# Moving one attention layer and several dense node layers to other passes of a fused four-network graph kernel

## What is computed

```python
# L0: graph attention, three layers
x = relu(node_features @ W0 + b0)
for l in range(3):
    # logits = leaky_relu(a_s[src] + a_d[dst] + ew); softmax over the edges of a node
    y = _gat(x, src_f, dst_f, ew_f, Wg[l], att_src[l], att_dst[l], bg[l], n)
    y = _layer_norm(y, gamma[l], beta[l])
    x = jax.nn.relu(x + y)
# L1: two graph convolutions (weighted), relu(agg @ W.T + b)
# L2: one graph convolution, relu(segment_sum(xw[row] * norm) + b)
# L3: two SAGE layers, relu(concat(h, mean of neighbours) @ W + b)
x = _layernorm(x + L0(x));  x = _layernorm(x + L1(x))
x = _layernorm(x + L2(x));  x = _layernorm(x + L3(x))
```

## Time and profile before

| what | value |
|---|---|
| median of 3 runs | 5088.15 us |
| the profiled execution's span | 5076.4 us |
| instructions | 107540 |
| busy: PE / DVE / ACT / POOL | 77% / 75% / 68% / 59% of the span |
| DMA packets | 606699, 1061.18 MB, mean 209 GB/s |
| `node_chain` | 860.9 us, DVE busy 798.2 |
| `edge_scores` 0, 1, 2 | 385.6, 316.8, 365.1 us |
| `convolve` 0, 1, 3 | 273.2, 260.7, 259.0 us |

### The profile page before, as it was taken

How to read it: one execution, slowest core, us unless ns; L and a number is a source line. 1 busy time by engine, 2 the same in 40 slices (tenths; PEclk the granted TensorE clock), 3 DMA queues, 4 the chain that set the end, 5 groups by cost and what they waited for, 6 DMA issues and landing times. The chain is left out here.

```text
span 5076.4 us, 107540 instructions
## 1 busy us (share of the span) xinstructions
PE 3921.6 (77%) x23992; PEld 2865.7 (56%) x23992; DVE 3818.0 (75%) x14850; ACT 3446.1 (68%) x11317; POOL 3017.8 (59%) x2914
## 2 busy tenths in 40 slices
PE   2999999565997798994998974997876676665554
PEld 1666766344775455773555752444765565665554
DVE  5899999676998787887886966997768787444443
ACT  0899999554886576784776863887878787333332
POOL 2888888475552122661223452887757676767777
PEclk9999999788998899997999997998999898997666
DMA  2566666587997576994776984775766566543332
GB/s 63 162 186 199 199 194 193 175 288 242 351 349 250 180 239 205 338 354 160 233 241 230 350 290 156 225 227 171 230 205 212 189 204 190 155 145 116 93 101 70
DMA packets 606699, 1061.18 MB, mean 209 GB/s; under 512 B 109737, under 2 KB 130875, under 8 KB 606509
## 3 DMA queue, kind: packets, MB, share of 16 engines
q1 hardware_dynamic: 524780, 920.61, 53.0%
q0 software_dynamic: 81728, 138.51, 10.7%
HBM read 608.75 MB, written 453.92 MB: 209 GB/s over the span
## 5 line engine op out<-in xcount | busy, mean ns | idle before, releaser
L2534 POOL DMA_INDIRECT got_c<-table,src_row x980 | 930.4, 949 | 387.6 <-issue 295.6
L1428 POOL DMA_INDIRECT src_got_s<-table,src_row x588 | 554.6, 943 | 452.9 <-PE bank L1474 105.1
L2566 PE MATMUL bank<-pick_c,got_c 128*128 128x128 f32 x1960 | 327.7, 319 | 349.6 <-DMA got_c<-table,src_row 271.2
L2076 PE MATMUL bank<-w_all,dt_m 128*128 128x512 f32 x1176 | 567.7, 599 | 35.0 <-DMA dt_m<-delta_t 33.4
L2566 PEld LDWEIGHTS bank<-pick_c,got_c 128*128 128x128 f32 x1960 | 284.2, 223 | 392.5 <-issue 233.5
L2050 POOL TENSOR_TENSOR part_m<-part_m,half_sum_m 128x512 f32<-128x512 f32 x98 | 158.7, 1619 | 580.3 <-DVE half_sum_m L2283 580.3
L1601 ACT ACTIVATE z_s<-z_s,shift_s,dev_s 128x128 f32<-128x128 f32 x1080 | 444.2, 486 | 1.8 <-DVE shift_s L1739 1.3
L791 PEld LDWEIGHTS bank<-w_mean,ht 128*128 128x128 f32 x2352 | 312.4, 193 | 142.9 <-issue 142.9
L2590 PE MATMUL bank<-w_c,agg_c 128*128 128x128 f32 x1960 | 365.4, 311 | 5.0 <-ACT agg_c L2711 4.7
L2711 ACT COPY agg_c<-bank 128x512 f32<-128x512 f32 x245 | 142.6, 582 | 325.4 <-DVE bank L1914 277.8
L788 PE MATMUL bank<-bias,first_row 128*128 128x512 f32 x588 | 321.8, 629 | 38.7 <-ACT ht L851 13.8
(11 more groups left out here) (352 smaller groups left out, 11925.4 us busy)
## 6 DMA issues: line engine op xcount, KB each, us to landing
table<-rows SPq DMA_DIRECT2D x294, 256.0 KB
x_s<-table SPq DMA_DIRECT2D x270, 256.0 KB
x_c<-table SPq DMA_DIRECT2D x245, 256.0 KB
table<-z_s SPq DMA_DIRECT2D x196, 256.0 KB
table<-z_c SPq DMA_DIRECT2D x196, 256.0 KB
table<-mid_s SPq DMA_DIRECT2D x172, 256.0 KB
own_rows_s<-table SPq DMA_DIRECT2D x147, 256.0 KB
pick_t_s<-picks_t SPq DMA_DIRECT2D x147, 256.0 KB
```

The source lines that it names most:

```text
L1428: nc.gpsimd.indirect_dma_start(out=src_got[r][:, g, :], out_offset=None, in_=tables[l].rows, in_offset=bass.IndirectOffsetOnAxis(ap=src_ro ...
L2076: nc.tensor.matmul(b_h[k % n_h][:, :], dt[b.slot][:, k, :], w_all[:, l, :, :].rearrange("p h d -> p (h d)"), start=True, stop=True).then_i ...
L2534: nc.gpsimd.indirect_dma_start(out=got[r][:, g, :], out_offset=None, in_=t_in.rows, in_offset=bass.IndirectOffsetOnAxis(ap=src_row[:, t:t ...
L2566: ins = nc.tensor.matmul(b_sum[r][:, k * P:(k + 1) * P], got[b.slot][:, k, :], pick[r][:, k, :], start=k == 0, stop=sage, skip_group_check ...
```

## The change

1. `node_chain` keeps the input layer and two attention layers. The addition of the old row (`add_rows`) goes from POOL to DVE for both, the bias of layer 1 is now copied into its bank by ACT (`set_bias`) instead of multiplied in by PE, and the steps of all engines are written in a new order with fewer steps between the stages of a batch. POOL issues its 392 node-map DMAs without pacing.
2. The third attention layer of the node rows, with the raw input added and the LayerNorm, goes into `edge_scores(0)` as its pair (`attention=...`, `row_deviation` on ACT, `layer_norm`, `residual`, `moments`, `scale` on DVE); it loads the old rows and the raw rows and writes t[3].
3. The pair of L1's two layers moves from `edge_scores(0)` to `edge_scores(1)`, that of L2's layer from `edge_scores(1)` to `edge_scores(2)`.
4. L3's node batches leave `edge_scores(2)`. All 98 now run in `convolve(0)` to `convolve(3)`: 25, 25, 25 and 23, one in every second pass. `convolve(0)` carries 25 as before.

```diff
+def node_quarters(nb):
+
+    hosted, n = (nb + 1) // 2, 2 * nb
+    starts = [min(k * hosted, n) for k in range(4)] + [n]
+    return list(zip(starts[:-1], starts[1:]))
...
-                        for n in range(n_batches + 7):
-                            if 7 <= n:
-                                add_rows(1, n - 7)
-                            if n < n_batches:
-                                hold(pool, first_made, n - 2)
-                                if n == nb:
-                                    pool.wait_ge(placed, 16 * n_tiles)
-                                map_step(4 * n)
-                            if 4 <= n < n_batches + 4:
-                                add_rows(0, n - 4)
-                            if n < n_batches:
-                                map_step(4 * n + 2)
+                        for t in range(n_tiles):
+                            place(t)
+                        pool.wait_ge(placed, 16 * n_tiles)
+                        for t in range(n_tiles):
+                            fetch(t)
                         pool.wait_ge(fetched, 16 * n_tiles)
 
...
+                        def add_rows(l, b):
+                            r = b.slot
+                            dve.wait_ge(y_read[l], b.count(1, 1))
+                            dve.wait_ge(rows_made[l], b.count(1, 1))
+                            nc.vector.tensor_tensor(flat(rows[l + 1][r]), flat(rows[l + 1][r]), flat(rows[l][r]),
+                                                    ALU.add).then_inc(summed[l], 1)
+
+                        def relu_rows(l, b):
+                            r = b.slot
+                            dve.wait_ge(summed[l], b.count(1, 1))
+                            nc.vector.scalar_tensor_tensor(rows[l + 1][r][:, :, :], rows[l + 1][r][:, :, :], 0.0, beta_k(l + 1), ALU.max,
+                                                           ALU.add).then_inc(made[l + 1], 1)
...
+                                scale(1, b)
+                                add_rows(1, b)
...
+                            if b:
+                                add_rows(0, b)
                                 relu_rows(0, b)
...
-        def edge_scores(l, first, second, t_in, t_mid, t_out, start, end, solo=False):
-            n_part, patch = end - start, l and not start
+        def edge_scores(l, first, second, t_in, t_mid, t_out, attention=None):
+            patch = l > 0
...
+                            if attention:
+                                sp.dma_start(flat(raw[h][b.slot]), batch_rows(io["x"], b.twin(h).batch())).then_inc(raw_in[h][b.slot], 16)
...
+                        def layer_norm(b, h):
+                            n = b.twin(h)
+                            dve.wait_ge(dev_made, n.count(1, 1))
+                            nc.vector.reciprocal(dev_y[h][:, :], dev_y[h][:, :]).then_inc(inverse, 1)
+                            dve.wait_ge(inverse, n.count(1, 1))
+                            hold(dve, z_stored[h][b.slot], b.ring4(16, -16))
+                            dve.sem_inc(dve_pace, 1)
+                            for g in range(GB):
+                                ins = nc.vector.scalar_tensor_tensor(z[h][b.slot][:, g, :], b_y[h][:, g * D:(g + 1) * D],
+                                                                     dev_y[h][:, g:g + 1], gamma_w[:, l + 2, :], ALU.mult, ALU.mult)
+                            ins.then_inc(y_read, 1)
+                            dve.wait_ge(y_read, n.count(1, 1))
+                            nc.vector.tensor_tensor(flat(z[h][b.slot]), flat(z[h][b.slot]), flat(x[h][b.slot]),
+                                                    ALU.add).then_inc(rows_added, 1)
...
+                        def step_attention(at):
+                            b = at(2)
+                            if b:
+                                difference(b)
+                            b = at(1)
+                            if b:
+                                layer_norm(b, 0)
+                                residual(b, 0)
+                                moments(b, 0)
+                            b = at(2)
+                            if b:
+                                scale(b, 1)
+                            b = at(1)
+                            if b:
+                                layer_norm(b, 1)
+                                residual(b, 1)
+                                moments(b, 1)
                                 scale(b, 0)
-                            b = at(2)
...
                 def even(b):
-                    return nodes and b and b.slot % 2 == 0
+                    if not nodes or not b or b.slot % 2:
+                        return False
+                    return not isinstance(b.i, int) or b.batch() // 2 < n_own
+
+                def node_batch(b):
+                    return b.ring(1, first_node - 1)
...
+                            b = at(5)
+                            if even(b):
+                                node_residual(b)
+                                node_moments(b)
+                            b = at(6)
+                            if even(b):
+                                node_scale(b)
...
-        edge_scores(0, (io["L1_gnn_W1"], io["c_L1_gnn_b1"]), (io["L1_gnn_W2"], io["b_L1_gnn_b2"]), t[3], t[4], t[5], 0, nb)
+        edge_scores(0, None, None, t[2], None, t[3], (w_mean[:, 2, :], bias[:, 2, :, :]))
         softmax(0)
         attend(0)
-        edge_scores(1, None, (io["L2_gnn_W"], io["b_L2_gnn_b"]), t[5], None, t[6], 0, nb)
+        edge_scores(1, (io["L1_gnn_W1"], io["c_L1_gnn_b1"]), (io["L1_gnn_W2"], io["b_L1_gnn_b2"]), t[3], t[4], t[5])
         softmax(1)
         attend(1)
-        middle = (nb + 1) // 2
-        third = (t[6], t[7], t[8], (io["L3_gnn_W1"][0:D, :], io["c_L3_gnn_b1"]), (io["L3_gnn_W2"][0:D, :], io["b_L3_gnn_b2"]))
-        edge_scores(2, third[3], third[4], *third[0:3], 0, middle)
-        edge_scores(2, third[3], third[4], *third[0:3], middle, nb, True)
+        edge_scores(2, None, (io["L2_gnn_W"], io["b_L2_gnn_b"]), t[5], None, t[6])
         softmax(2)
         attend(2)
-        convolve(0, "gcn0", False, t[3], t[4], None, (io["L1_gnn_W1"],), io["b_L1_gnn_b1"], third + (2 * (nb - middle) + 1,))
-        convolve(1, "gcn0", True, t[4], t[5], t[3], (io["L1_gnn_W2"],), io["b_L1_gnn_b2"])
-        convolve(2, "gcn1", True, t[5], t[6], t[5], (io["L2_gnn_W"],), io["b_L2_gnn_b"])
-        convolve(3, "sage", False, t[6], t[7], None, (io["L3_gnn_W1"][D:, :], io["L3_gnn_W1"][0:D, :]), io["b_L3_gnn_b1"])
+        third = (t[6], t[7], t[8], (io["L3_gnn_W1"][0:D, :], io["c_L3_gnn_b1"]), (io["L3_gnn_W2"][0:D, :], io["b_L3_gnn_b2"]))
+        quarters = [third + (lo, hi) for lo, hi in node_quarters(nb)]
+        convolve(0, "gcn0", False, t[3], t[4], None, (io["L1_gnn_W1"],), io["b_L1_gnn_b1"], quarters[0])
+        convolve(1, "gcn0", True, t[4], t[5], t[3], (io["L1_gnn_W2"],), io["b_L1_gnn_b2"], quarters[1])
+        convolve(2, "gcn1", True, t[5], t[6], t[5], (io["L2_gnn_W"],), io["b_L2_gnn_b"], quarters[2])
+        convolve(3, "sage", False, t[6], t[7], None, (io["L3_gnn_W1"][D:, :], io["L3_gnn_W1"][0:D, :]), io["b_L3_gnn_b1"], quarters[3])
         convolve(4, "sage", True, t[7], t[8], t[6], (io["L3_gnn_W2"][D:, :], io["L3_gnn_W2"][0:D, :]), io["b_L3_gnn_b2"])
```

530 lines of the change are left out of this document (201 added, 329 removed).

## The result

The changed kernel takes 5452.26 us (median of 4 runs, 5447.98 to 5454.08), the kernel before 5087.38 beside it. The ratio is 1.072, 95% interval 1.0707 to 1.0733. Forecast were 5210 us and a range of 5120 to 5300: the sign was right, the size was not, 365 us slower instead of 122.

The account below looks back on a forecast made before the run. Limits differed by block: busy PE, DVE and ACT in node_chain, transfers in the scores, gathers and almost a DVE-ACT ring in convolve(1). Terms -209 + 124 + 73 - 48 + 85 + 85 + 12 = +122 gave 5210 us, range 5120 to 5300.

Parts of the forecast that it names:

- `node_chain`: Term for this block: 6.35 us per batch by VectorE's list, 652 us in all, -209.
- rival 3: node_chain bound by its round of waits at the lower clock, 7.7 us per batch, total 5348 us; chance 0.12.
- `edge_scores(0)`: Term for this block: VectorE's list sets 10.0 us per pass, 510 us in all, +124.
- `edge_scores(1)` and `(2)`: Terms for these blocks: transfer-bound before and after, 390 us (+73) and 316.75 us (-48).
- `convolve(1)` and `(2)`: Terms for these blocks: node batches enter the DVE and ACT ring, mean 6.37 us per pass, 346 us each, +85 each.
- The ring of the earlier trace: In convolve(1), DVE and ACT wait on each other with nothing spare; with node batches it sets 6.37 us per pass.
- `convolve(3)`: Term for this block: node batches cost fill and drain only, about +12 us.
- 1 and 2: Rivals: everything moved is hidden, 4944 us, chance 0.04; only the convolutions hide, 5068 us, 0.06 shared with the cheap-ends rival.
- the four: All rivals: everything hidden, only convolutions hidden, node_chain's round at lower clock, and all terms at cheap ends together (5055 us).
- The clock, weighed for `node_chain`: With PE idler in node_chain its clock may fall to the lower level, 138 us more than forecast; chance 0.12.

Follow-up runs that it names:

- Experiment 8: GpSimd adds the rows in edge_scores(0) beside VectorE's statistics and aggregation, ACT normalises behind the next squares, against the base: 5124.63 us, 1.0079 of before.
- Experiment 6: VectorE's shift in convolve(1) and (2) one step later, ACT's node steps ahead of its normalisations, against the base: 5215.24 us beside 5218.52.
- experiment 1: In convolve(3) of the changed kernel, ACT sets the bias and copies the sums out ahead of its node steps: 5217.59 us, 1.0262 of before.
- experiment 3: In convolve(0) of the changed kernel, the copy of the sums one step later, as in convolve(3): 5621.14 us (one run).
- experiments 7: GpSimd adds the rows in edge_scores(0) between its gathers, against the base: 5433.28 us; reordered 6402.64 and 6398.35; with VectorE's difference first again 5312.47.
- the base: The changed kernel with ACT's copy of the sums ahead of its node steps in convolve(3): 5218.52 us, 1.0258 of before.

## Why the prediction was wrong, point by point

**`node_chain`: right.** 654 for 652 us. VectorE's hidden-layer add and max, L891, in 300 us of the changed kernel:

```profile
300.00:600.00 300.00, 37.63 (x47) 1.00 0.52 168
```

47 batches, 6.38 us each, for 6.35; at a clock of 0.98 although PE was busy 75% of the block instead of 91%. So rival 3 (round at the lower clock) fell. That it is VectorE's list and not the round beside it was not tried.

**`edge_scores(0)`: the number right, its reason only half.** 511 for 510, 30 passes in 300 us. But the sum took VectorE's 10.0 us as a list with small overlaps and forecast it busy over 90%, and VectorE was busy 434 of 511 us (85%), 8.9 per pass. Experiment 8 brought the pass to 8.0 us by taking 1.4 from the list and 0.6 of waits with it. So some of the 10.0 us was order and not work; that the sum met it was partly luck.

**`edge_scores(1)` and `(2)`: right**, within 5 us, at a DMA share of 0.95 in both, for 0.96 and 0.95 in the blocks whose place they took the earlier trace rows.

**`convolve(1)` and `(2)`: nearly right**, +95 for +85. The period is 6.84 us, worked out from the window below (152/4 = 38 aggregations in 260 us), for 6.37; fill and drain are 20 us, for 34. The intervals between VectorE's reciprocals (L2777, 3801 to 3857 us) are in turn 6.2 and 7.6 us on average, where 5.9 and 6.8 were forecast: the pass that was mis-sized most is the odd one, by 0.8 us. Periods too short by 23 us in all met a fill too long by 14, so the +85 is nearer than its terms.

```profile
3790.00:4050.00 260.00, 14.41 (x152) 0.91 0.68 213
```

The ring of the earlier trace rows was named as the cause. Experiment 6 cut it and gained nothing that can be measured, so the ring was at most one of two bounds. The other is probably ACT's list, 303 busy of 353 us and 223 of 250 in the middle; the forecast had seen ACT only as the ring's partner.

**`convolve(3)`: wrong, and it is the whole miss.** The step that failed reads "DVE 125 and ACT 83 of 259 us leave room, so as in `convolve(0)` the node batches cost fill and drain only". The busy shares did leave room; experiment 1 shows that the batches cost 2 us once the order allows it. What the step left out is the order itself. For `convolve(1)` I had walked round the ring instruction by instruction, for `convolve(3)` I took over the result of another block by its busy times. The two blocks share the code of their node steps but differ in one number, `b = at(2 if sage else 1)`, which stands in the code before (and in where PE's `add_own` stands, which made no ring: with the number alone changed, experiment 3 made it in `convolve(0)`). `convolve(1)` and `(2)` have `at(2)` too, but there ACT copies the sums ahead of its node steps, the order that experiment 1 gave to `convolve(3)`. With ACT's and PE's order of a step side by side the round would have been seen: node product, ACT's node copy, `sums_out`, product, next sums, next node product. Its length could have been summed too, as experiment 3's expectation does for `convolve(0)`: 7.6 us per pass at full clock, up to 10 with the clock that follows; 8.3 were measured there (49 relus start from 3486.7 to 3886.8 us).

**The rivals.** 1 and 2 (all or the convolutions hidden) were refuted by the blocks' own times. None of the four was the one that came: a ring in the block with the most room. The clock, weighed for `node_chain`, fell elsewhere: in `convolve(3)`, where PE stood waiting in every pass, from 0.98 to 0.75. Around the rows shown it is 1.00 while PE ends its node product and stands (4664 to 4668 us), and 0.50, the lower of its two levels, in the product behind a wait (4658 to 4660 and 4670 to 4672). That agrees with "activity releases the throttle" in the Trainium skill ("TensorE: Matmul & The Clock Gate", "Part 1: The HAM clock gate (the "warmup" mystery)"); `node_chain`, where PE became idler and kept 0.98, shows nothing of it. PE's busy share of `convolve(3)` would not have foretold it: 66% before and after. It was a consequence: in experiment 1 it rose to 0.97 with no edit to PE.

## What to carry to other kernels

When work is hosted beside other work, room in busy time is not enough. Write the step of each engine down in order and look for a pair of engines that wait for each other within one step; if there is one, the pass takes the sum of both sides, however idle both are. The cure is one step of distance, or the short thing that others wait for ahead of the thing that waits. And when a new order makes all engines idler at once and the clock falls with them, look for the ring first: here the clock came back by itself once the ring was cut. When a period is taken from a count in a window, divide the time between the first and the last start, not the window.

## What the runs showed of the hardware

GpSimd's addition of two tensors (128x512, 1.26 us) held off VectorE's shift, which reads two tensors of SBUF: 1.24 to 1.25 us instead of 0.16, 50 times of 50. It did not hold off statistics and aggregation, which read one (0.86 and 0.38 us with and without it). The Trainium skill says in "SBUF — State Buffer", section "SBUF: two separate sides", that the port pair which VectorE and GpSimd share "is an **exclusive lock**, not a bandwidth split": of a VectorE instruction with two inputs in SBUF and a GpSimd instruction that reads SBUF, the one that starts first has it to its end. The traces of experiments 7 and 8 agree: the addition began at 1403.95 us, the shift at 1403.98, and the shift ended with the addition. So work may be moved from VectorE to GpSimd, if it is placed beside the right neighbours: the same additions made the block 97 us slower in one order and 92 us faster in another, the second with ACT's normalisation moved too.

Twice the kernel before, run beside experiments 6 and 7, took 5686 and 5684 us, 12% more than elsewhere. In the first of these, in the profiled run of experiment 6, `node_chain` took 1138 us for 654 and `convolve(0)` 338 for 274; from 100 to 750 us its transfers ran at 39 GB/s on average for 158 in the base, with stretches of 1 to 2 GB/s. Why is open. It is not a fixed trait of a chip as far as the record tells: the second time and experiment 8 bear the same chip number, 11, and there the kernel before took 5684 us and later 5087. A time says something only beside its base, run at the same time on the same chip.
